# Last attention of a four-block network: ScalarE in place of GpSimd divides the probabilities of six of the 32 steps

## Chip, cores and metric

One core of one Trainium2 chip runs the whole program in one launch. The metric is the device time of that launch in microseconds (us), lower is better. The engines are TensorE (PE, with its weight loads as PEld), VectorE (DVE), ScalarE (ACT), GpSimd (POOL) and SyncE (SP), which issues DMAs. They run their own instruction lists and meet at semaphores.

## The reference, cut to what matters

Eight blocks follow each other on x of 4 x 256 rows by 256 columns; the change is in the seventh, the eighth comes behind it and its router is interleaved with the seventh.

```python
x = x + _L3_xattn_ref(_layernorm(x), ctx_2048, itok_BxS_0_1023, ...)   # 16 heads of 128
    scores = (q_nope . k_nope + q_rope . k_rope) * scale
    good = (k_ids <= qs) & (k_ids >= qs - LOOKBACK)                     # each query sees few keys
    attn = jax.nn.softmax(jnp.where(good, scores, NEG), axis=-1)        # exp, then divided by its sum
    out = einsum(attn, v); x += out @ W_o
x = x + _L3_ffn_ref(_layernorm(x), ...)      # 64 experts, each row goes to 8 of them:
    top_k of x @ gate_w, rows gathered by expert, silu(gate) * up, down, weighted sum
```

## The kernel before

The last attention (function `l3x`) makes 32 steps, each for two heads and 256 queries. It is a software pipeline over k = 0 to 73: every engine has a loop over k that says what it does at k, and all engines run through these loops side by side. In the text "step q" is an attention step (q = 0 to 31), and k is the position in the pipeline. A step is spread over some ten values of k:

- TensorE: the query of step q at k = 2q (18 matrix products, L349 to L351 reading `qch`), the scores at k = 2q + 3 (L2650), four transposes of the probabilities at k = 2q + 8 (`tensor_turn`, L2658), the product with the values at k = 2q + 9 (`tensor_out`, L2668), and the output projection at k = 2q + 11 (`tensor_y`, L349 to L351 reading `op6h`).
- VectorE: the rotary part of the query (L2750 to L2753), mask and row minimum of the scores (`vector_masked`, L2762), at k = 2q + 5 the reciprocals of the sums (`ri6n`, L2785), and the low part of the heads (L2776). For the last two steps (q = 30, 31; the constant OWN is 30) it also divides (L2789).
- ScalarE: copy of the query (L2710), exponentials in four pieces of 128 x 128, two at k = 2q + 3 and two at k = 2q + 4 (L2715), copy of the transposed probabilities from PSUM to SBUF (`pt6n`, L2728) at k = 2q + 8, and the high part of the heads (`op6h`, L2732) at k = 2q + 9.
- GpSimd: at k = 2q + 5 it waits for the reciprocals of step q and divides, that is, it multiplies four 128 x 128 pieces of `p6n` in place by `ri6n` (L2839), for q = 0 to 29. The probabilities lie in five buffers used in turn.

`tensor_turn(k)` waits for the division of its step; then `pt` is copied, and `tensor_out` waits for that copy. In the order of TensorE only the scores of a later step stand between the transposes and `tensor_out`.

Between these the router of the eighth block runs for each of four groups of 256 rows as the rows of x get done: groups 0 to 2 inside this stage. For group g it starts at k = 26 + 16g: normalization (VectorE, with `rs` of L396 on GpSimd), transposes (L3242), copy `hT` on ScalarE (L3249), router logits on TensorE (L3273), mask `mk` and slots on VectorE, counts on TensorE (L3298 to L3303), row weights on VectorE (L3394). GpSimd then scatters the rows of the group to the experts' slots in HBM, with 16 indirect DMAs per group (`gpsimd_scatters`, L3357, `slots_in`): the table of the loop puts one or two of them at each k from 38 for group 0 and from 54 for group 1, behind the division of that k. In order, five scatters fall on two steps of attention. The 32 scatters of groups 2 and 3 follow from k = 70 on and in the next stage (`head`), where TensorE runs dense experts; then the gathered experts start, once all 64 scatters have landed.

Of the kernel before, what the change touches and what calls it, by code (L numbers as in the profile page):

```python
# [14 lines left out]
ACT = mybir.ActivationFunctionType  # L15
# [19 lines left out]
OWN = 30  # L35
# [2545 lines left out]
def l3x(nc, io, m, sig):  # L2581

    T, V, A, G, B = nc.tensor, nc.vector, nc.scalar, nc.gpsimd, m.B
    prev_norm = m.norm
    x = m.x = sig("x", NT)
    done = m.xfinal = lambda t: x.at(t + 1)
    m.next_norm = Norm(nc, m, sig, rows=m.row7[:, :, 0:D])
    r, w7 = m.router, m.weights = Router(nc, io, m, sig), Weights(nc, io, m, sig)
    done = m.xfinal
# [4 lines left out]
    sc, mn, ri, tr, pt, pn = [sig(n, c) for n, c in (  # L2594
        ("scores", 32), ("masked", 64), ("recip", 32), ("probs_T", 32), ("probs_T_sbuf", 32), ("probs_p", OWN))]
    ex, pnv = sig("exps", 64), sig("places", 32 - OWN)
    pv, oh, ol, y = [sig(n, 32) for n in ("heads", "heads_hi", "heads_lo", "heads_out")]
    m.heads_read = ol.at(32)
    m.queries_done, m.y_done = qlat.at(32), y.at(32)
# [2 lines left out]
    def routing(k):  # L2602

        g = (k - 26) // 16
        return g, k - 25 - 16 * g
# [28 lines left out]
    def tensor_score(k):  # L2634
# [15 lines left out]
                    i = T.matmul(B[2 + s][:, c], m.Q6[k % 2][r, j, c], K[r, w], start=(j == 0), stop=(j == 1))  # L2650
        i.then_inc(sc.sem, 1)

    def tensor_turn(k):
        T.wait_ge(*(pn.at(k + 1) if k < OWN else pnv.at(k + 1 - OWN)))
        if k >= 1:
            T.wait_ge(*pt.at(k))
        for i in range(4):
            r = T.transpose(B[4][:, i * 128:i * 128 + 128], m.p6n[k % 5][:, i, :], m.ident[:])  # L2658
        r.then_inc(tr.sem, 1)
# [23 lines left out]
    def tensor():  # L2683
        for k in range(74):
            if 0 < k < 64 and k % 2 == 0:
                tensor_query(k // 2)
            if k in (69, 70, 71):
                beat(T, m, B[1][:, 256:384], 3)
            if 8 <= k < 72 and k % 2 == 0:
                tensor_turn(k // 2 - 4)  # L2690
            if 3 <= k < 67 and k % 2:
                tensor_score((k - 3) // 2)
            if 9 <= k < 73 and k % 2:
                tensor_out((k - 9) // 2)
            if k >= 11 and k % 2:
                tensor_y((k - 11) // 2)
            if k >= 26:
                g, ago = routing(k)
                if g == 0 and ago == 5:
                    T.wait_ge(*m.joined.at(4))  # L2700
                if ago == 5:
                    r.tensor_turn(g, bank)
                if ago == 7:
                    r.tensor_logits(g, bank)
                if ago == 9:
                    r.tensor_count(g, bank)

    def scalar_query(q):
        A.wait_ge(*qlat.at(q + 1))
        A.copy(m.Q6[q % 2][:, 1, :], B[1][:, 0:256]).then_inc(qlh.sem, 1)  # L2710

    def scalar_exp(q, s):
        A.wait_ge(*mn.at(2 * q + s + 1))
        for i in (2 * s, 2 * s + 1):
            a = A.activation(m.p6n[q % 5][:, i, :], m.sc6n[q % 3][:, i, :], ACT.Exp, bias=m.mn6n[q % 5][:, i:i + 1],  # L2715
                             scale=-1.0, accum_out=m.su6n[q % 5][:, i:i + 1])
        a.then_inc(ex.sem, 1)

    def scalar():
        for k in range(74):  # L2720
            if 64 <= k < 67:
                scalar_exp((k - 3) // 2, (k - 3) % 2)
            if 0 < k < 64 and k % 2 == 0:
                scalar_query(k // 2)
            if 8 <= k < 72 and k % 2 == 0:
                q = k // 2 - 4
                A.wait_ge(*tr.at(q + 1))
                A.copy(m.pt6n[q % 3][:].rearrange("p s n -> p (s n)"), B[4][:]).then_inc(pt.sem, 1)  # L2728
            if 9 <= k < 73 and k % 2:
                q = (k - 9) // 2  # L2730
                A.wait_ge(*pv.at(q + 1))
                A.copy(m.op6h[q % 2][:], B[6][:, 0:256]).then_inc(oh.sem, 1)  # L2732
            if 3 <= k < 64:
                scalar_exp((k - 3) // 2, (k - 3) % 2)
            if k >= 26:
                g, ago = routing(k)
                if ago == 6:
                    r.scalar_turned(g, bank)
                if ago == 9:
                    r.scalar_exps(g)  # L2740
                if ago == 11:
                    r.scalar_high(g)
            if k in (12, 16, 20, 24):
                w7.scalar_high(k // 4 - 3)
# [86 lines left out]
    def gpsimd():  # L2831
        r.gpsimd_small()
        for k in range(74):
            if 5 <= k < 5 + 2 * OWN and k % 2:
                q = (k - 5) // 2
                G.wait_ge(*ri.at(q + 1))
                for i in range(4):
                    p = m.p6n[q % 5][:, i, :]
                    a = G.tensor_scalar(p, p, m.ri6n[q % 5][:, i:i + 1], 1.0, ALU.mult, ALU.mult)  # L2839
                a.then_inc(pn.sem, 1)  # L2840
            if k in (13, 17, 21, 25):
                w7.gpsimd_low(k // 4 - 3)
            if k == 24:
                r.gpsimd_places()
            if k >= 26:
                g, ago = routing(k)
                if ago == 2:
                    r.norm.gpsimd_rstd(g)
                if ago >= 13:
                    r.gpsimd_scatters(g, ago - 13)  # L2850
                elif g:
                    r.gpsimd_scatters(g - 1, ago + 3)

    return {"tensor": tensor, "scalar": scalar, "vector": vector, "gpsimd": gpsimd, "sync": sync}


# [1152 lines left out]
def program(nc, io, ctx):  # L4009
    m, sig = Mem(), Signals(nc, ctx)  # L4010
    memory(nc, ctx, m)
    m.slots_used = True
    stages(nc, io, m, sig, l0x, keys, l3p, l3x)
    for engine in (nc.scalar, nc.gpsimd, nc.tensor, nc.sync, nc.vector):
        engine.wait_ge(*m.fit.at(1))
    fit = nc.values_load(m.fit7[0:1, 0:1], min_val=0, max_val=1)
    value = reached(dict(sig.value))
    with nc.If(fit == 1):
        for part in few(nc, io, m, sig).values():
            part()  # L4020
    sig.value = {name: value.get(name, 0) for name in sig.sems}
    with nc.Else():
        for part in again(nc, m, sig).values():
            part()
        m.slots_used = False
        stages(nc, io, m, sig, l0x_wide, keys_wide, l3p_wide, l3x_wide)
        for part in every(nc, io, m, sig).values():
            part()
# [131 lines left out]
```

## Time and profile before

| | us |
|---|---|
| median of 3 runs | 686.11 (685.12 to 688.25) |
| profiled execution | 685.7 |
| its span | 683.0 |
| TensorE busy | 609.0 (89%) |
| VectorE busy | 523.7 (77%) |
| ScalarE busy | 428.1 (63%) |
| GpSimd busy | 363.0 (53%) |

The profiled execution's time is 2.7 us above its span (what lies before the first and after the last instruction). Starts are counted from the start of the span. The attention stage runs from about 300 to 446 us. "Idle before" in a row is the time that the engine stood still ahead of that instruction, and the name behind the arrow is what ended it.

### The profile page before, as it was taken

What the parts mean: (1) busy time and instruction counts of PE and PEld (TensorE: products, weight loads), DVE (VectorE), ACT (ScalarE), POOL (GpSimd) and SP (SyncE); (2) the same over time, 40 slices, a digit from 0 to 9 for tenths busy, and PEclk for the clock granted to TensorE, in tenths of its full rate; (3) what the DMA queues carried; (4) which work ended last, traced back from release to release, by engine and by line L of the source; (5) the groups of instructions that cost most, each with busy time, mean ns of one, the idle gap of its engine ahead of it and who ended that gap; (6) DMA issues with size and microseconds to landing.
All of it is one profiled execution on the core that took longest, in us unless ns stands there. A gap on an engine that the chain in (4) does not pass through costs nothing.

```text
span 683.0 us, 14285 instructions
## 1 busy us (share of the span) xinstructions
PE 609.0 (89%) x4996; PEld 508.8 (74%) x5000; DVE 523.7 (77%) x1534; ACT 428.1 (63%) x1150; POOL 363.0 (53%) x524
## 2 busy tenths in 40 slices
PE   3998979898899879989999999897799989988877
PEld 3977867776589834668888878675599888888764
DVE  6494489989856788687778988778778878878466
ACT  3635578949745368767776666452358878868430
POOL 6615848964600225435543888677405665666620
PEclk9999999999999999999999999999799999999998
DMA  8999023200010050039300112534448878876384
GB/s 318 334 300 300 27 58 106 82 2 1 4 47 1 0 231 1 2 95 368 114 2 10 66 67 83 183 135 154 159 146 280 261 263 292 282 251 216 133 344 168
DMA packets 47701, 100.50 MB, mean 147 GB/s; under 512 B 7390, under 2 KB 27951, under 8 KB 46246
## 3 DMA queue, kind: packets, MB, share of 16 engines
q1 hardware_dynamic: 40374, 82.33, 36.0%
q0 software_dynamic: 7248, 17.18, 6.8%
q8 instruction: 42, 0.69, 0.4%
q14 instruction: 37, 0.30, 0.2%
HBM read 60.04 MB, written 43.12 MB: 151 GB/s over the span
## 4 chain that ended last, share of the span: by engine, by line
PE 59%; DVE 19%; POOL 8%; ACT 7%; issue 6%; another core or an unknown queue 0%; DMA 0%; DVEq 0%; ACTq 0%; POOLq 0%
PE bank L349 13%; PE bank L351 12%; PE bank L350 11%; PE bank L2650 4%; PE bank L3707 3%; PE bank L2668 3%; PE bank L2658 2%; POOL hl L1238 2%; DVE st L382 2%; DVE HN L402 2%; DVE pt L1451 1%; DVE nm L1459 1%; PE bank L3790 1%; PE bank L1574 1%; POOL raw L1329 1%
## 5 line engine op out<-in xcount | busy, mean ns | idle before, releaser
L3946 POOL DMA_INDIRECT rows_out<-ye,di x87 | 91.4, 1051 | 65.0 <-issue 19.3
L3357 POOL DMA_INDIRECT slots_in<-row,si x64 | 65.6, 1026 | 25.1 <-issue 17.2
L349 PE MATMUL bank<-x7h,w7h 128*96 128x192 f32 x232 | 63.0, 272 | 10.5 <-DVE h L3885 5.7
L2839 POOL TENSOR_SCALAR p6n<-p6n,ri6n 128x128 f32<-128x128 f32 x120 | 46.1, 401 | 46.2 <-DVE ri6n L2785 45.8
L349 PE MATMUL bank<-w7h,h7h 96*128 96x256 f32 x164 | 49.7, 303 | 14.8 <-DVE X L3496 9.4
L351 PE MATMUL bank<-x7h,w7l 128*96 128x192 f32 x232 | 59.1, 255 | 0.3 <-issue 0.2
L350 PE MATMUL bank<-x7l,w7h 128*96 128x192 f32 x232 | 59.0, 254 | 0.0
L2715 ACT ACTIVATE p6n<-sc6n,mn6n 128x128 f32<-128x128 f32 x128 | 50.4, 397 | 10.8 <-DVE mn6n L2762 10.4
L396 POOL TENSOR_TENSOR rs<-ve,neghalf 128x2 f32<-128x2 f32 x32 | 23.1, 721 | 59.4 <-DVE ve L390 59.1
L3180 DVE TENSOR_TENSOR w7l<-w7f,w7h 128x640 fp32r<-128x640 f32 x60 | 49.5, 826 | 4.2 <-issue 2.3
L349 PEld LDWEIGHTS bank<-x7h,w7h 128*96 128x96 f32 x232 | 38.0, 164 | 13.9 <-DVE w7l L3180 8.9
L350 PE MATMUL bank<-w7l,h7h 96*128 96x256 f32 x164 | 47.6, 290 | 0.8 <-issue 0.8
L3803 ACT CAST x7h<-bank 128x384 fp32r<-128x384 f32 x58 | 27.8, 482 | 32.5 <-PE bank L3707 28.7
L351 PE MATMUL bank<-w7h,h7l 96*128 96x256 f32 x164 | 47.7, 291 | 0.0
L3175 ACT CAST w7h<-w7f 128x640 fp32r<-128x640 f32 x64 | 47.2, 740 | 0.0
L349 PEld LDWEIGHTS bank<-w7h,h7h 96*128 96x128 f32 x164 | 32.3, 197 | 16.5 <-DVE X L3496 7.7
L3813 ACT ACTIVATE ye<-bank,wd 128x256 f32<-128x256 f32 x87 | 38.8, 485 | 8.9 <-PE bank L351 7.0
L3846 DVE TENSOR_TENSOR x7l<-bank,x7h 128x384 fp32r<-128x384 f32 x58 | 31.7, 548 | 16.1 <-ACT x7h L3803 14.0
L2762 DVE CUSTOM_DVE_ANT_0 sc6n<-bank,nm 128x128 f32<-128x128 f32 x128 | 29.4, 285 | 13.6 <-PE bank L2650 13.6
L351 PEld LDWEIGHTS bank<-x7h,w7l 128*96 128x96 f32 x232 | 38.0, 164 | 0.3 <-issue 0.3
L350 PEld LDWEIGHTS bank<-x7l,w7h 128*96 128x96 f32 x232 | 38.1, 164 | 0.0
L1441 ACT ACTIVATE p<-bank,nm 128x256 f32<-128x256 f32 x64 | 29.6, 483 | 9.4 <-DVE nm L1459 9.2
(483 smaller groups left out, 2247.0 us busy)
## 6 DMA issues: line engine op xcount, KB each, us to landing
w7f<-in_w SPq DMA_DIRECT2D x64, 320.0 KB
xe<-slots_in SPq DMA_DIRECT2D x29, 432.0 KB
slots_in<-zt SPq DMA_DIRECT2D x7, 1728.0 KB, 17.9
rows_out<-zt SPq DMA_DIRECT2D x8, 1024.0 KB, 11.1
rw<-rows_out SPq DMA_DIRECT2D x3, 2048.0 KB
w0raw<-in_w SPq DMA_DIRECT2D x3, 768.0 KB
wo<-in_w_o SPq DMA_DIRECT2D x1, 2048.0 KB
raw<-in_w SPq DMA_DIRECT2D x2, 704.0 KB
```

The costliest lines, as they stand in the source:

```text
L349: T.matmul(out, lh, rh, start=first, stop=False, **kw)
L350: T.matmul(out, lh, rl, start=False, stop=False, **kw)
L351: return T.matmul(out, ll, rh, start=False, stop=last, **kw)
L1441: a = A.activation(m.p2[n][:, mc, :], B[2 * (k % 2) + i % 2][:, mc * 256:mc * 256 + 256], ACT.Exp, bias=m.nm2[n][:, mc:mc + 1], accum_out= ...
L2715: a = A.activation(m.p6n[q % 5][:, i, :], m.sc6n[q % 3][:, i, :], ACT.Exp, bias=m.mn6n[q % 5][:, i:i + 1], scale=-1.0, accum_out=m.su6n[q ...
L2839: a = G.tensor_scalar(p, p, m.ri6n[q % 5][:, i:i + 1], 1.0, ALU.mult, ALU.mult)
L3175: A.copy(self.high(e)[:], self.whole(e)).then_inc(self.hi.sem, 1)
L3180: V.tensor_tensor(self.low(e)[:], self.whole(e), self.high(e)[:].bitcast(F32), ALU.subtract).then_inc(self.lo_v.sem, 1)
L3357: G.indirect_dma_start(out=m.buf_in, out_offset=bass.IndirectOffsetOnAxis(ap=m.si7[:, t, j:j + 1], axis=0), in_=m.row7[:, t, :], in_offset ...
L3813: A.activation(m.ye7[q % NY][:], out_bank(q), ACT.Copy, scale=m.wd7[:, 0, q:q + 1]).then_inc(ye.sem, 1)
L3846: V.tensor_tensor(m.x7l[j % 3][:, c, :], B[c][:, 0:2 * CAP], m.x7h[j % 3][:, c, :].bitcast(F32), ALU.subtract).then_inc(xl.sem, 1)
L3946: G.indirect_dma_start(out=m.buf_out, out_offset=bass.IndirectOffsetOnAxis(ap=m.di7[:, q:q + 1], axis=0), in_=m.ye7[q % NY][:], in_offset= ...
```

## The change

Six steps, q = 18, 20, 22, 24, 26 and 28, are divided by ScalarE, with four activations (Copy with a scale per row) at k = 2q + 6, right behind the exponentials of that k. GpSimd leaves out its division there. The transposes of a step wait for whichever engine divides it, by a semaphore of its own for ScalarE.

```diff
+    by_scalar = tuple(range(18, OWN, 2))
+    pna = sig("probs_scalar", len(by_scalar))
...
+    def normalized(k):
+        if k >= OWN:
+            return pnv.at(k + 1 - OWN)
+        done = sum(q <= k for q in by_scalar)
+        return pna.at(done) if k in by_scalar else pn.at(k + 1 - done)
+
     def tensor_turn(k):
-        T.wait_ge(*(pn.at(k + 1) if k < OWN else pnv.at(k + 1 - OWN)))
+        T.wait_ge(*normalized(k))
...
                 scalar_exp((k - 3) // 2, (k - 3) % 2)
+            if k % 2 == 0 and (k - 6) // 2 in by_scalar:
+                q = (k - 6) // 2
+                A.wait_ge(*ri.at(q + 1))
+                for i in range(4):
+                    a = A.activation(m.p6n[q % 5][:, i, :], m.p6n[q % 5][:, i, :], ACT.Copy,
+                                     scale=m.ri6n[q % 5][:, i:i + 1])
+                a.then_inc(pna.sem, 1)
...
-            if 5 <= k < 5 + 2 * OWN and k % 2:
+            if 5 <= k < 5 + 2 * OWN and k % 2 and (k - 5) // 2 not in by_scalar:
```

GpSimd's order from step 17 on (buffer `p6n2` is step 17, `p6n3` 18, `p6n4` 19, `p6n0` 20, `p6n1` 21, `p6n2` 22, `p6n3` 23; "DMA slots_in" are the scatters of group 0), before:

```order
L2839 TENSOR_SCALAR p6n2_299<-p6n2_299,ri6n2_314 128x128 x4
L3357 DMA slots_in<-row7_364,si7_381 13312x288 x2
L2839 TENSOR_SCALAR p6n3_300<-p6n3_300,ri6n3_315 128x128 x4
L3357 DMA slots_in<-row7_364,si7_381 13312x288 x3
L2839 TENSOR_SCALAR p6n4_301<-p6n4_301,ri6n4_316 128x128 x4
L396 TENSOR_TENSOR rs_59<-ve_58,neghalf_55 128x2
L3357 DMA slots_in<-row7_364,si7_381 13312x288 x2
L2839 TENSOR_SCALAR p6n0_297<-p6n0_297,ri6n0_312 128x128 x4
L3357 DMA slots_in<-row7_364,si7_381 13312x288 x3
L2839 TENSOR_SCALAR p6n1_298<-p6n1_298,ri6n1_313 128x128 x4
```

and now:

```order
L2854 TENSOR_SCALAR p6n2_299<-p6n2_299,ri6n2_314 128x128 x4
L3372 DMA slots_in<-row7_364,si7_381 13312x288 x5
L2854 TENSOR_SCALAR p6n4_301<-p6n4_301,ri6n4_316 128x128 x4
L396 TENSOR_TENSOR rs_59<-ve_58,neghalf_55 128x2
L3372 DMA slots_in<-row7_364,si7_381 13312x288 x5
L2854 TENSOR_SCALAR p6n1_298<-p6n1_298,ri6n1_313 128x128 x4
```

The scatters of two steps, which stood as two and three between divisions, now stand as five in a row; the same happens from step 21 to 23 and from 25 to 29.

ScalarE's order at k = 62 to 64, the last place of the change, before:

```order
L2728 COPY pt6n0_317<-bank4 128x512
L2715 ACTIVATE p6n4_301,su6n4_311<-sc6n2_296,mn6n4_306 128x128 x2
L2732 CAST op6h1_285<-bank6 128x256
L2715 ACTIVATE p6n0_297,su6n0_307<-sc6n0_294,mn6n0_302 128x128 x2
L3249 COPY hT32_363<-bank5 128x2x256
L2715 ACTIVATE p6n0_297,su6n0_307<-sc6n0_294,mn6n0_302 128x128 x2
```

and now:

```order
L2736 COPY pt6n0_317<-bank4 128x512
L2723 ACTIVATE p6n4_301,su6n4_311<-sc6n2_296,mn6n4_306 128x128 x2
L2747 ACTIVATE p6n3_300<-p6n3_300,ri6n3_315 128x128 x4
L2740 CAST op6h1_285<-bank6 128x256
L2723 ACTIVATE p6n0_297,su6n0_307<-sc6n0_294,mn6n0_302 128x128 x2
L3264 COPY hT32_363<-bank5 128x2x256
L2723 ACTIVATE p6n0_297,su6n0_307<-sc6n0_294,mn6n0_302 128x128 x2
```

The division of step 28 (L2747) stands ahead of the high part of the heads, two exponentials and the router's copy `hT`. At the other five places it stands likewise between the exponentials and `op6h`. The orders of TensorE, VectorE and SyncE are the same as before.

## Rows read from the trace of the kernel before

**Rows 1.** The page: engines' busy time, and the chain that ended last
```profile
PE 609.0 (89%) x4996; PEld 508.8 (74%) x5000; DVE 523.7 (77%) x1534; ACT 428.1 (63%) x1150; POOL 363.0 (53%) x524
...
PE 59%; DVE 19%; POOL 8%; ACT 7%; issue 6%; another core or an unknown queue 0%; DMA 0%; DVEq 0%; ACTq 0%; POOLq 0%
```
**Rows 2.** Three stretches: PE, PEld, DVE, ACT, POOL busy (instructions), TensorE clock, DMA
```profile
305.00:372.00 67.00, 67.00 (x648) 56.41 (x646) 51.57 (x248) 50.09 (x189) 32.44 (x78) 1.00 0.39 134
372.00:440.00 68.00, 63.37 (x582) 52.34 (x579) 58.04 (x269) 43.41 (x165) 55.35 (x87) 0.97 0.29 100
```
**Rows 3.** TensorE's waits, 375 to 445 us: total, times, longest
```profile
PE bank L2668 <- ACT pt6n L2728: 2.5, 4, 0.9
PE bank L3298 <- DVE mk L3288: 1.8, 1, 1.8
PE bank L3273 <- ACT hT L3249: 0.4, 1, 0.4
...
PEld bank L2658 <- POOL p6n L2839: 0.2, 1, 0.2
```
**Rows 4.** Chain of work, 396 to 407 us: start, length, what
```profile
398.73 1.09 PE bank L2650 x16
...
402.13 0.12 PE bank L350
402.25 1.61 PE bank L351
403.86 0.02 issue
403.89 0.37 ACT Q L2710
404.26 0.50 ACT pt6n L2728
404.75 0.04 issue
404.80 0.65 PE bank L2668 x4
```
**Rows 5.** GpSimd in order of time: start, length, instruction, [idle before]
```profile
378.54 1.42 POOL L2839 TENSOR_SCALAR p6n<-p6n,ri6n 128x128 f32<-128x128 f32 x4 [0.16 <-DVE ri6n L2785]
...
400.35 1.05 POOL L3357 DMA_INDIRECT slots_in<-row,si  x1 [0.17 <-issue]
...
402.97 0.96 POOL L3357 DMA_INDIRECT slots_in<-row,si  x1 [0.30 <-issue]
...
430.89 1.42 POOL L2839 TENSOR_SCALAR p6n<-p6n,ri6n 128x128 f32<-128x128 f32 x4
...
437.63 0.96 POOL L3357 DMA_INDIRECT slots_in<-row,si  x1 [0.30 <-issue]
441.73 0.96 POOL L3357 DMA_INDIRECT slots_in<-row,si  x1 [3.14 <-DVE row L3394]
```
**Rows 6.** ScalarE in order of time where step 28's division will stand
```profile
425.74 0.39 ACT L2715 ACTIVATE p6n<-sc6n,mn6n 128x128 f32<-128x128 f32 x1
426.03 0.19 ACT L2715 ACTIVATION_READ_ACCUMULATOR p6n<-sc6n,mn6n 128x1 f32 x1
426.98 0.37 ACT L2732 CAST op6h<-bank 128x256 fp32r<-128x256 f32 x1 [0.76 <-PE bank L2668]
...
428.03 0.57 ACT L3249 COPY hT<-bank 128x512 f32<-128x512 f32 x1
```
**Rows 7.** ScalarE: `op6h` behind steps 18, 20, 22, 24, 26, with its idle time
```profile
382.16 0.37 ACT L2732 CAST op6h<-bank 128x256 fp32r<-128x256 f32 x1 [1.14 <-PE bank L2668]
...
390.70 0.37 ACT L2732 CAST op6h<-bank 128x256 fp32r<-128x256 f32 x1 [0.76 <-PE bank L2668]
...
400.77 0.35 ACT L2732 CAST op6h<-bank 128x256 fp32r<-128x256 f32 x1
...
409.68 0.37 ACT L2732 CAST op6h<-bank 128x256 fp32r<-128x256 f32 x1 [0.40 <-PE bank L2668]
...
417.77 0.37 ACT L2732 CAST op6h<-bank 128x256 fp32r<-128x256 f32 x1 [0.32 <-PE bank L2668]
```
**Rows 8.** TensorE in order of time, steps 28 and 29
```profile
427.68 0.60 PE L2658 MATMUL bank<-ident,p6n 128*128 128x128 f32 x4
428.65 1.10 PE L3273 MATMUL bank<-rg,hT 128*128 128x64 f32 x8 [0.37 <-ACT hT L3249]
...
432.37 0.66 PE L2658 MATMUL bank<-ident,p6n 128*128 128x128 f32 x4
434.87 0.48 PE L3298 MATMUL bank<-base,ones 1*128 1x128 f32 x2 [1.84 <-DVE mk L3288]
```
**Rows 9.** Chain of work, 426 to 446 us
```profile
429.75 1.86 PE bank L2650 x16
...
438.06 1.68 PE bank L2658 x4
```
**Rows 10.** VectorE in the next stage, where scatters run without a break
```profile
488.09 0.88 DVE L3496 SCALAR_TENSOR_TENSOR X<-bank,wt,X 128x256 f32<-128x256 f32 x2 [2.43 <-PE bank L351]
```

## Prediction

> **What bounds the kernel now.** I read the page first [rows 1]: TensorE is busy for 609.0 of 683.0 us and makes 59% of the chain that ended last; ScalarE (63% busy, 7% of the chain) and GpSimd (53%, 8%) have room on the average. An average says little of one stage, so next come the stretches [rows 2]. From 305 to 372 us, attention without scatters, TensorE is busy for 67.00 of 67.00 us: nothing else matters there. From 372 to 440 us, where the scatters run and all six changed steps lie, it is busy for 63.37 of 68.00, so 4.6 us stand open. GpSimd is the busy one beside it: 55.35 of 68.00 us, against 32.44 of 67 before. ScalarE has 43.41 of 68.
>
> Then the waits of TensorE [rows 3], which say who owns those 4.6 us. The division on GpSimd is waited for once, by a weight load, for 0.2 us. The rest is 2.5 us in four waits of `tensor_out` for the copy `pt6n`, 1.8 us once for the router's mask `mk` on VectorE, 0.4 us once for the router's copy `hT` on ScalarE. So the work that the change takes off GpSimd is nearly never what TensorE waits for.
>
> What makes `pt6n` late is not ScalarE's own load either. The chain [rows 4] shows one of the four: matmuls follow each other at 0.12 us, but the last one of the query stands with 1.61 us, until 403.86; only then can ScalarE copy `Q` and `pt6n`, and TensorE goes on at 404.80. TensorE's own end signal came some 1.5 us late. There is nothing of this in the 67.00 full microseconds before the first scatter, and at 400.35 to 403.9 GpSimd is issuing scatters [rows 5]. The scores at 429.75 are drawn out likewise, 1.86 us in place of 1.09 [rows 4, 9], and the transposes at 438.06 with 1.68 us. I call these **late signals**. They come while GpSimd issues scatters; the rows do not say by which path.
>
> **The change part by part.**
>
> *GpSimd, removed:* six divisions of 1.42 us [rows 5], 8.5 us of its 55.35. TensorE waits for none of these six. Step 29's division, which stays, is the one behind the 0.2 us wait: it starts at 430.89 and its transposes follow at 432.37 [rows 5, 8]. Without step 28's division ahead it starts up to 2 us earlier. That buys nothing: TensorE's next work at 434.87 waits for `mk` for 1.84 us anyway [rows 8], so 0.2 us more of idle time go there. The scatters of group 1, which end at 438.6 now, end some 2 us earlier; group 2 starts at 441.73 and waits 3.14 us for the row weights of VectorE [rows 5]. Credit: 0.
>
> *ScalarE, added:* four activations of 128 x 128 per step. No row shows a Copy with a scale per row on this shape. The exponential on the same shape lasts 0.39 us, and its follower starts 0.29 us behind it [rows 6]. I take 0.30 us each, since they follow back to back, so 1.2 us per step; bounds are 0.26 (nothing but a shorter start) and 0.39 each (no overlap), 1.0 to 1.6 us per step. The page ScalarE: Activation LUTs of the Trainium skill (Rules for kernel authors) speaks against the change: it gives multiplications to VectorE and budgets about 0.3 us per activation and 0.83 ns per element. As an estimate from that page a step is 4 x 0.41 = 1.6 us, and the sum below would be +0.9 in place of +0.45. The row's 0.29 us from start to start decides for me.
>
> What hides the 1.2 us: the division stands between the exponentials and `op6h`, and there ScalarE stands idle for 1.14, 0.76, 0, 0.40 and 0.32 us at steps 18 to 26 [rows 7], and 0.76 us at step 28 [rows 6]. So `op6h` comes 0.1 to 1.2 us later. `op6h` itself has time (its reader, `tensor_out` of the next step, is over 3 us away); the tight one is the copy `pt6n` behind it, which has 1.09 us of scores to hide its 0.50 us [rows 4]. Ahead of it lies ScalarE's second idle place, the wait for the query (part of the 0.4 to 2 us that it waits each step for TensorE). At steps 18, 20, 24 and 26 the rest, 0.1, 0.45, 0.8 and 0.9 us, ends there or in the 0.5 us of cover. At step 22 the whole 1.2 us stays, but the query of 402.25 is late by 1.5 us just there, so it is hidden too. Credit: 0 for five steps.
>
> At **step 28** something else stands behind the division: `hT`. TensorE waits for that copy already (0.37 us, [rows 8]), because at k = 64 no query is left to compute. `hT` starts at 428.03 and would start 1.2 - 0.76 = 0.45 us later; logits, scores, mask, counts follow from it one after the other. This is **+0.45 us** on the path.
>
> *The new wait of the transposes:* step 28's division ends on ScalarE at 426.22 + 1.2 = 427.4 us (426.22 is the end of the accumulator read [rows 6]), the transposes start at 427.68 [rows 8]. It holds by 0.25 us; behind it in TensorE's list stand the logits, which wait for `hT` later than that. With 0.39 us per piece it ends at 427.8 and costs nothing more.
>
> *Late signals:* scatters that stood as two and three between divisions now stand as five. Now the five pairs of steps with two-and-three cost, by the four waits of 2.5 us less the last one of 0.46 us, plus 0.77 us of the scores, 2.8 us in all, so 0.56 us per five scatters. The one existing run of five (432.48 to 438.6) costs 0.46 us: the wait behind the transposes of 438.06. Moved to that price the five pairs give 5 x (0.46 - 0.56) = **-0.5 us**. The bounds are far apart: all 3.3 us gone, or much more (below). The page SBUF — State Buffer of the Trainium skill (Who interferes with whom) says that a DMA never contends with a compute engine and that TensorE and ScalarE wait for no one. By that rule the grouping of scatters is worth nothing and the sum is +0.45. The rows speak against it at least for signals, 1.61 us in place of 0.12.
>
> *Everything else* (experts behind 446 us, blocks before 300 us) is unchanged in order. **Sum:** +0.45 - 0.5 = -0.05, about 0. On the profiled execution's 685.7 us that is 685.65, and the median of the runs stands 0.4 above it, so I predict **686.0 us** for the median. A measurement of this kernel can tell about 0.5%, 3.4 us, from no change.
>
> **The rivals.**
>
> *A, slower: longer runs of scatters hold TensorE's signals longer.* For it: in the next stage, where scatters follow each other without a break, VectorE waits 2.43 us for a matmul [rows 10] whose neighbours take a quarter of a microsecond. Against it: run of five at 432 to 438 cost only 0.46 us, and the ten scatters from 441.73 on hold nothing that the waits show. Place: `pt6n` and the masks from 378 to 431 us. Price: a signal held for 2.4 us leaves 2.4 - 0.6 = 1.8 us of stall (0.9 of 1.5 us came through at 404.80), against 0.56 now, so +1.26 us per run, five runs: +6.3 + 0.45, **692.9 us**. It decides as slower from three runs of five on (+4.2). Chance 0.14.
>
> *B, faster: fewer turns between division and scatter, no late signals.* The 3.3 us of stall go and `hT` costs 0.45: **683.2 us**. The half microsecond that TensorE would keep by not falling in speed behind its wait at 434.87 could add to it. For it: late signals are denser from 378 to 431 us than from 441 to 457. Against it: scatters are the same in number. Chance 0.11.
>
> *C, ScalarE becomes the bound.* With 1.6 us per step and no lucky late query, steps 20, 22, 24 and 26 overrun the cover of `pt6n` by 0.1 to 0.4 us each, and step 28 costs 0.85: +2.0 - 0.5, **687.6 us**. For it: no idle time ahead of `op6h` at step 22. Against it: ScalarE is busy for 64% of the stretch [rows 2], with 7.2 us more 75%. Chance 0.09.
>
> **How the numbers follow.** The forecast has 0.66. Its own range is 684.2 to 687.8 (late signals coming and going by one or two). With the rivals the range is 682.9 to 689.2: A is in it as long as two runs or fewer show it, B and C wholly. Faster by over 0.5%: half of B (when more than the stalls goes) and 0.01 of the forecast, 0.07. Slower: A from three runs on, 0.07, and 0.02 of the others, 0.09. Within 0.5%: 0.84.
>
> **What the profile after would show.** Four ACT activations `p6n<-p6n,ri6n` per changed step at about 0.3 us from start to start; `hT` of group 2 starting 0.4 to 0.5 us later against the transposes of step 28, and TensorE's wait for it 0.8 us in place of 0.4; no wait for POOL `p6n`; GpSimd idle ahead of its divisions of steps 19 to 29; waits for `pt6n` of 1.5 to 3.5 us in total. Wrong would be: waits for `pt6n` over 6 us (A) or under 1 us (B), or `pt6n` late with the query's signal on time (C).

## The result, and the profile after

| | before | changed |
|---|---|---|
| median of the runs | 686.5 us (685.12 to 688.25, 4 runs) | 698.89 us (698.04 to 700.84, 4 runs) |
| profiled execution, its span | 685.7, 683.0 us | 698.53, 695.8 us |
| ratio | | 1.0178, 95% interval 1.0146 to 1.0210 |

The change makes the kernel 12.4 us slower. The forecast was 686.0 us, with a range to 689.2. I start with the page of the changed kernel, to be held against [rows 1]:

```profile
PE 613.6 (88%) x4996; PEld 511.3 (73%) x5000; DVE 524.1 (75%) x1534; ACT 432.9 (62%) x1174; POOL 353.9 (51%) x500
...
PE 49%; DVE 22%; ACT 10%; POOL 8%; issue 7%; another core or an unknown queue 3%; DMA 0%; DVEq 0%; ACTq 0%; POOLq 0%
```

GpSimd has lost 9 us of work and ScalarE gained 5. Neither is near its limit. What is new is in the chain: 3% of it, 21 us, stand as "another core or an unknown queue" on a kernel with one core. That is time behind a signal which came after the instruction that raised it had ended.

Next the stretches of the changed kernel, for [rows 2], with two more (columns as there):

```profile
305.00:372.00 67.00, 66.94 (x646) 56.16 (x644) 51.52 (x247) 50.20 (x191) 32.59 (x78) 1.00 0.39 134
372.00:440.00 68.00, 59.09 (x507) 48.82 (x507) 50.68 (x233) 42.88 (x167) 37.98 (x55) 0.92 0.20 71
376.00:456.00 80.00, 67.56 (x572) 55.69 (x569) 57.70 (x259) 47.39 (x181) 42.56 (x59) 0.91 0.24 85
385.00:388.00 3.00, 3.00 (x16) 2.83 (x14) 2.29 (x9) 1.93 (x8) 2.81 (x6) 0.50 0.00 0
```

The last two of them in the kernel before:

```profile
376.00:456.00 80.00, 75.19 (x642) 60.94 (x639) 65.62 (x289) 49.38 (x169) 63.48 (x92) 0.98 0.31 108
385.00:388.00 3.00, 2.54 (x20) 2.16 (x21) 2.97 (x16) 2.41 (x10) 2.50 (x4) 1.00 0.07 24
```

Up to 372 us nothing differs. From 376 to 456 us TensorE is busy for 7.6 us less, and its granted clock is 0.91 in place of 0.98; just behind its first long wait it is 0.50, which is the lower of its two levels, 1.2 GHz. To see where it adds up I use one landmark, the transposes of step 31, the last of the attention. They start at 442.46 us before, and in the changed kernel at:

```profile
455.10 0.60 PE L2666 MATMUL bank<-ident,p6n 128*128 128x128 f32 x4
```

That is 12.6 us later. From there to the end both traces take the same, 240.5 and 240.7 us. So the whole loss arises in the stretch that the change touches. Over the same work, from 376 us to this landmark, TensorE is idle for 4.8 us before and 12.4 now, and busy for 61.7 and 66.7. So 7.6 us of the loss is idle time, and the other 5.0 us is the same work at the lower clock.

TensorE's waits from 375 to 456 us in the changed kernel, for [rows 3]:

```profile
PE bank L2676 <- ACT pt6n L2736: 8.6, 5, 3.2
...
PE bank L3313 <- DVE mk L3303: 2.0, 1, 2.0
...
PE bank L3288 <- ACT hT L3264: 1.2, 2, 0.8
...
PE bank L2666 <- ACT p6n L2747: 0.3, 1, 0.3
```

`pt6n` was 2.5 us. Two of the five waits make most of it: 3.2 us behind the first row of five scatters and 3.1 us behind the fourth; behind the second it is 1.2, behind the third 0.2. The first is shown here, and it is the model of them. GpSimd in the changed kernel, with five scatters where two, a division and three had been:

```profile
375.78 1.05 POOL L3372 DMA_INDIRECT slots_in<-row,si  x1 [0.17 <-issue]
...
380.94 1.21 POOL L3372 DMA_INDIRECT slots_in<-row,si  x1 [0.30 <-issue]
384.66 1.41 POOL L2854 TENSOR_SCALAR p6n<-p6n,ri6n 128x128 f32<-128x128 f32 x4 [2.51 <-DVE ri6n L2800]
```

TensorE and ScalarE at the same time:

```profile
378.75 0.60 PE L2666 MATMUL bank<-ident,p6n 128*128 128x128 f32 x4
...
380.06 0.39 PE L2652 MATMUL bank<-KL,Q 64*128 64x128 f32 x4
383.62 0.65 PE L2676 MATMUL bank<-pt6n,KC 128*64 128x256 f32 x4 [3.18 <-ACT pt6n L2736]
```

```profile
381.54 0.37 ACT L2718 COPY Q<-bank 128x256 f32<-128x256 f32 x1 [2.98 <-remote]
382.99 0.58 ACT L2736 COPY pt6n<-bank 128x512 f32<-128x512 f32 x1 [1.07 <-remote]
...
384.25 1.27 ACT L2747 ACTIVATE p6n<-p6n,ri6n 128x128 f32<-128x128 f32 x4
385.42 0.35 ACT L2740 CAST op6h<-bank 128x256 fp32r<-128x256 f32 x1
```

The transposes end at 379.35; `pt6n`, which needs nothing but them and a free ScalarE, starts at 382.99, 0.8 us behind the last scatter's end (382.15). From 378.56 to 382.99 ScalarE does nothing but the copy of `Q`, and its four new activations come only later, so they can't be the reason. The signal of the transposes was held for 3.6 us. "Remote" is how the profile names such a wait.

### The profile page after: what moved, and what is told of

Its sections match the earlier page's. It is cut to its first block, busy times and chain, and to the rows that moved or that the text cites. A ratio compares the mean times of both kernels' runs of the same rounds, so it can differ in the third digit from the quotient of the medians.

```text
span 695.8 us, 14285 instructions
## 1 busy us (share of the span) xinstructions
PE 613.6 (88%) x4996; PEld 511.3 (73%) x5000; DVE 524.1 (75%) x1534; ACT 432.9 (62%) x1174; POOL 353.9 (51%) x500
## 4 chain that ended last, share of the span: by engine, by line
PE 49%; DVE 22%; ACT 10%; POOL 8%; issue 7%; another core or an unknown queue 3%; DMA 0%; DVEq 0%; ACTq 0%; POOLq 0%
PE bank L349 11%; PE bank L351 10%; PE bank L350 9%; PE bank L2652 3%; PE bank L3722 3%; PE bank L2676 2%; DVE st L382 2%; POOL hl L1238 2%; DVE HN L402 1%; ACT ye L3828 1%; DVE w7l L3195 1%; PE bank L2666 1%; DVE pt L1451 1%; ACT p6n L2723 1%
## 5 line engine op out<-in xcount | busy, mean ns | idle before, releaser
L3961 POOL DMA_INDIRECT rows_out<-ye,di x87 | 94.4, 1085 | 60.6 <-issue 17.9
L2854 POOL TENSOR_SCALAR p6n<-p6n,ri6n 128x128 f32<-128x128 f32 x96 | 34.7, 378 | 60.1 <-DVE ri6n L2800 60.1
```

Source lines behind the costliest of these rows:

```text
L3961: G.indirect_dma_start(out=m.buf_out, out_offset=bass.IndirectOffsetOnAxis(ap=m.di7[:, q:q + 1], axis=0), in_=m.ye7[q % NY][:], in_offset= ...
```

## The experiments

**Is it ScalarE's load, or the gap in GpSimd's?** Four kernels, beside which the kernel before took 686.64 us.

`e1_fill` is the change, with a dummy in place of each division that went:

```diff
+            if k % 2 and (k - 5) // 2 in by_scalar:
+                G.wait_ge(*ri.at(q + 1))
+                for i in range(4):
+                    a = G.tensor_scalar(m.spare[n % 2][:, i, :], m.ident[:], m.ri6n[q % 5][:, i:i + 1], ...)
```

> ScalarE divides the six steps as in the change, and GpSimd, where its divisions were, multiplies a constant tile into a spare buffer that nobody reads, with the same wait for the reciprocals and the same four 128 x 128 instructions. So ScalarE's load is that of the change and the scatters stand again as two and three. Theory A (runs of five scatters hold TensorE's signals): back to the kernel before, 685 to 688 us, waits for pt6n 1.5 to 4 us in place of 8.6. Rival (ScalarE's load, or its division coming too late, is what costs): it stays at 697 to 700 us.

Measured: 686.76 us (10 runs), ratio 0.9996 (0.9971 to 1.0021). The whole loss is gone, with ScalarE's divisions still in place.

`e3_act` is the reverse: the kernel before, with four idle Copy activations on ScalarE at the same six places (`A.activation(m.spare[0][:, i, :], m.ident[:], ACT.Copy, scale=...)`).

> The kernel before, with four activations (Copy with a scale per row, 128 x 128, from a constant tile into a spare buffer) on ScalarE at each of the six places of the change; GpSimd divides everything as before. Theory A: 686 to 688 us, the 1.2 us are hidden but for some 0.5 us at step 28. Rival (ScalarE's load): 697 to 700 us.

Measured: 688.35 us (10 runs), 1.0003 (0.9978 to 1.0028). ScalarE's new load costs nothing that these runs can show; the interval leaves room for 1.9 us. (The ratios come with the measurement and are not always the quotient of the two medians, which is 1.0025 here.)

`e2_vector` gives the six divisions to VectorE (`if q >= OWN or q in by_scalar:` in its own division of the last steps), so that ScalarE has none and GpSimd the same rows of five.

> VectorE divides the six steps (one 128 x 512 instruction of 0.69 us each, as it does for the last two steps), ScalarE divides nothing, GpSimd is as in the change. Theory A: runs of five scatters are still there, 695 us or more. Rival (ScalarE's load): 684 to 688 us, like before.

Measured: 693.31 us, 1.0102 (1.0066 to 1.0138). The loss needs no ScalarE. It is smaller than the change's. TensorE's wait for `pt6n` is 4.2 us in four here, none over 1.3, and its clock at 385 to 388 us stays at 1.00. Its longest wait is 2.5 us, for `hT`. How much of this loss is VectorE's, which has six divisions more, this run does not tell.

`e4_one` gives ScalarE a single step: `by_scalar = (18,)`, so one row of five.

> The change for one step alone, q = 18: one run of five scatters in place of a two and a three. Theory A with a cost per run: about a fifth of the 12.4 us, 688 to 690 us, with one wait for pt6n of about 2 to 3 us at 380 to 385 us. Rival (ScalarE's load summed over six steps): a sixth, also about 688 us, but then the wait stands behind ScalarE's division and not ahead of it. If only the last place (hT, step 28) or a loss behind the attention counted: 686 us.

Measured: 694.63 us, 1.0118 (1.0078 to 1.0159). One row of five costs 8 of the 12.4 us. The first line is TensorE's wait, the second its window behind it (TensorE alone: busy, clock, DMA share, GB/s):

```profile
PE bank L2676 <- ACT pt6n L2736: 3.9, 2, 3.2
```

```profile
385.00:388.00 3.00, 3.00 (x16) 0.50 0.00 0
```

It is the same 3.2 us and the same half clock. Of the 8 us, 5.7 are there at the transposes of step 31 (448.19 us in this trace, 442.46 before): 2.8 us are more idle time of TensorE (all its waits from 375 to 456 us, 7.5 in place of 4.7), and 3.0 us is the same work at the lower clock. Up to here: the cause is GpSimd's row of scatters, and the first place alone costs more than half of the whole.

**A place where nothing happens.** Four more kernels, meant as doses.

`e5_quarter`: as `e1_fill`, but the dummy is one piece of 128 x 128 in place of four.

> The change, with a break of one 128 by 128 multiplication (a quarter of the division's work, an estimate of 0.36 us) on GpSimd at the six places where a division was, behind the same wait for the sums' reciprocals. If only the length of an unbroken run of scatters counts, and any pause lets TensorE's held signals through, this reads like the kernel before, 685 to 688 us. If the queue of signals needs the time that it takes after the last scatter in the change's trace (about 0.8 us), the break lets part of them through, and the time lies between, 689 to 696 us. If the wait for the reciprocals itself, and not the work, was the break, it would read 686 too, and the idle time of GpSimd ahead of the dummy shows it.

`e6_signals`: the kernel before, where TensorE raises three more signals in each step:

```diff
+    extra = sig("extra", 96)
...
-        mm3(T, B[0][:, 0:256], ..., True, True)
+        mm3(T, B[0][:, 0:256], ..., True, True).then_inc(extra.sem, 1)
```

> The kernel before, with three more signals of TensorE in each of its steps (after the first query product, the first half of the scores and the first half of the values), for which nobody waits; the arithmetic and all waits stay. Theory of a queue, in which TensorE's signals are let through about one per scatter while GpSimd issues scatters: nine signals a step in place of six make the queue longer, the signals that are waited for arrive later, and the kernel is slower with no change on GpSimd, 692 to 705 us. Theory of a hold in time (each signal is late by what is left of the run, whatever stands before it): no change, 685 to 688 us. An increment may also cost TensorE itself something; then the steps ahead of the scatters (before 372 us) lengthen as well.

`e7_even`: the kernel before, with one scatter in each half step; `e8_even_after`: the change with the same:

```diff
-        for i in range(min(16, step * 5 // 4), min(16, (step + 1) * 5 // 4)):
-            self.gpsimd_scatter(g, i)
...
+        elif step < 16:
+            self.gpsimd_scatter(g, step)
```

(The branch of this attention is shown. One scatter of group 2 more is left to the head stage, whose loop is moved by one.)

> The kernel before, with one scatter in each half step in place of five in four half steps: between two divisions stand always two scatters, never three, and four of them lie further back, the last ones in the head stage. Theory of the run's length: the holds get shorter, the waits of TensorE in the later half of the attention (4.7 us from 375 to 456 us in the kernel before) shrink to 2 or 3 us, and the kernel takes 683 to 686 us, unless the later scatters put the load of the gathered rows off, which would give back up to 3 us. Rival: the run of three is short enough already, 686 to 689 us.

> The change, with one scatter in each half step: where a division is gone, four scatters stand in a row in place of five. A dose between the two kernels. If the queue grows with the run, this takes 689 to 696 us; if there is a length past which the stall sets in all at once, it reads like the one kernel or like the other (686 or 699 us).

Measured: 656.9, 656.96, 656.61 and 656.1 us. All are within 0.2% of the kernel before (ratios 0.9993, 0.9999, 0.9999 and 0.9989), and the kernel before itself took **657.09 us** here, in 31 runs (655.2 to 659.3). The same program took 682 to 687 us in every other batch, and the record gives the same chip number, 9, for this batch and for the first four kernels. TensorE's waits from 375 to 456 us in `e7_even`:

```profile
PE bank L3298 <- DVE mk L3288: 1.4, 1, 1.4
PE bank L349 <- DVE op6l L2776: 0.9, 1, 0.9
PE bank L2668 <- DVE op6l L2776: 0.5, 1, 0.5
```

No wait for `pt6n` is left. I compared the end of every instruction that raises a signal with the time at which the trace has the signal. In the profiled execution of the kernel before, 96 of TensorE's 661 signals are recorded more than 0.3 us late. None of them lies before 377 us, and GpSimd issues its first DMA of the whole program at 372.9. Of the other engines no signal is recorded late. But in that trace nearly 200 signals of VectorE, over 180 of ScalarE, 50 of TensorE and 27 of GpSimd have no record of their own before the engine's next one. In most of these cases an instruction that waits on that semaphore started in between, so these look like gaps in the record and not like late signals. In `e5_quarter` to `e8_even_after` no signal at all is late, and at most six in a trace have no record. Their scatters take as long as before (1.04 us in `e5_quarter`). So the holding of signals is a state, there in this batch or not for all runs alike, and not a property of the program. Two windows in the experts stage show that the two states differ beyond the attention too: TensorE alone, `e7_even` first, then the kernel before:

```profile
490.00:640.00 150.00, 147.04 (x1329) 0.98 0.81 281
```

```profile
500.00:650.00 150.00, 135.78 (x1237) 0.99 0.71 234
```

The step-31 landmark is at 437.57 in `e7_even`, 4.9 us ahead of 442.46; the other 24.5 us of the difference in span come behind it. That held signals make all of these 24.5 us is not shown. For the change this batch says something plain: with its six divisions on ScalarE and rows of four or of two and three scatters, nothing is lost or won. The change as it is did not run here, so that its own rows of five cost nothing in this state is likely, not shown.

**Again, where signals are held.** Beside the next two kernels the kernel before took 682.43 us.

`e9_again` is the changed kernel once more.

> The change as it is, once more, beside the kernel before on one chip. The last four kernels ran where the kernel before takes 657 us and where no signal of TensorE, VectorE or ScalarE comes later than 0.3 us in the attention; the change was measured where it takes 686 us and many come late. If the held signals are the whole cause of the 12 us, the change costs nothing wherever the kernel before takes about 657 us (ratio 0.997 to 1.004), and 1.014 to 1.021 wherever it takes about 686 us. If something else is at work, the ratio is the same in both.

Measured: 691.49 us, 1.0151 (1.0093 to 1.0209): the loss is back. Not every stall comes back in its size. Behind the first row of five TensorE waits 1.6 us in place of 3.2, and its clock stays at 1.00 there; behind the fourth it is 3.0. From the transposes of step 17 to those of step 31 this trace takes 72.2 us, the first one of the same program 76.4, and the kernel before 63.4. One wait of one trace is good to a factor of two.

`e10_signals` is `e6_signals` once more.

> The kernel before with three more signals of TensorE in each step, as in e6_signals. Where the kernel before takes about 657 us it shows nothing again. Where it takes about 686 us: by the theory of a queue that lets about one signal through per scatter it is slower, 692 to 705 us; by the theory of a hold in time it stays at 685 to 688 us.

Measured: 682.11 us (10 runs), 1.0013 (0.9979 to 1.0047). Three more signals in each step change nothing. The theory that the signals stand in a queue which lets one through per scatter falls; in this trace four of TensorE's signals arrive within 0.2 us of each other, 0.6 to 0.8 us behind the end of a row. These were held together and let go together. Not all are: in the first row of the changed kernel four late signals arrive at 378.57, 380.08, 381.52 and 382.96 us, one behind each scatter, 0.5 to 0.9 us behind its end. So a signal can come through in the middle of a row, or be held to its end.

**How long a row, how long a break.** Four kernels, beside which the kernel before took 685.56 us.

`e11_quarter` and `e12_even_after` are `e5_quarter` and `e8_even_after` once more.

> As e5_quarter: the change, with one multiplication of 128 by 128 (0.38 us in that trace) on GpSimd where a division was. Where signals are held (the kernel before at 680 to 690 us): if any break is enough, the ratio is 0.997 to 1.004; if the held signals need the time that they took after the last scatter of a row (about 0.8 us), part of the loss stays, 1.005 to 1.013; if the length of the break doesn't matter at all but its work does, as the change, 1.015 to 1.02. Where nothing is held (657 us), no difference.

> As e8_even_after: the change, with four scatters in a row in place of five. Where signals are held: 1.005 to 1.013 if the loss grows with the row's length, 1.0 or 1.018 if it has a threshold.

Measured: 692.56 us, 1.0100 (1.0060 to 1.0140), and 691.96 us, 1.0093 (1.0062 to 1.0124). Both keep about half of the loss. For `e11_quarter` this means that a break of 0.38 us between two and three scatters does only half of what one of 1.42 us does. For `e12_even_after` it does not mean that four in a row cost half of what five do, for it carries a second change, a longer row at the end of the attention. From the transposes of step 17 to those of step 29, where its rows of four lie, it takes 56.3 us, the kernel before 53.3 and the changed kernel 65.7 (64.7 in `e9_again`): the rows of four cost a quarter of what the rows of five do. Another 3.1 us go between steps 29 and 31, where seven scatters stand in a row and TensorE then waits for 3.05 us:

```profile
441.81 1.12 PE L2676 MATMUL bank<-pt6n,KC 128*64 128x256 f32 x4 [3.05 <-issue]
```

The first row of four, in GpSimd's order, and the wait of TensorE behind it:

```profile
376.03 1.06 POOL L3372 DMA_INDIRECT slots_in<-row,si  x1 [0.17 <-issue]
...
379.93 0.96 POOL L3372 DMA_INDIRECT slots_in<-row,si  x1 [0.31 <-issue]
```

```profile
382.71 0.65 PE L2676 MATMUL bank<-pt6n,KC 128*64 128x256 f32 x4 [2.03 <-ACT pt6n L2736]
```

`e13_woven` weaves the first scatter of a half step into the division (`if i == 1 and early: r.gpsimd_scatter(*early[0])` between its heads).

> The kernel before, with the first scatter of each half step that has a division put between the second and the third head of that division, so that rows of two and three scatters become rows of one and two. The division's end, for which TensorE waits, comes 1.3 us later. If the length of the row is what holds the signals, TensorE waits less, 0.988 to 0.998 of the kernel before where signals are held; where nothing is held only the later division is left, 1.000 to 1.006. If each scatter holds by itself, whatever stands around it, it is 1.000 to 1.006 in both.

Measured: 687.69 us (10 runs), 1.0029 (1.0009 to 1.0049). Shorter rows do what they should: six of TensorE's signals are late in the attention in place of 22, and its waits for `pt6n` fall to 0.4 us from 2.5. But from step 17 to step 29 the trace takes 56.4 us in place of 53.3, with waits for other things, the division (1.0 us) and the router's normalized rows (1.4 us) among them, and only from step 29 to 31 it is ahead (6.6 in place of 10.1). The later division takes back what the shorter rows give.

`e14_even` is `e7_even` once more.

> As e7_even: the kernel before, with rows of two scatters, never three. Where signals are held: 0.993 to 0.999 by the theory of the row's length; by its rival, that three in a row are short enough already, 0.999 to 1.004.

Measured: 690.50 us, 1.0077 (1.0053 to 1.0101), against my expectation. But look where. The landmark of step 31 stands at

```profile
438.27 0.60 PE L2658 MATMUL bank<-ident,p6n 128*128 128x128 f32 x4
...
446.31 1.12 PE L2668 MATMUL bank<-pt6n,KC 128*64 128x256 f32 x4 [6.77 <-ACT pt6n L2728]
```

4.2 us ahead of the kernel before. Of that, 1.5 us was there before the first scatter; from step 17 on it is 2.7 us ahead (60.7 us in place of 63.4, and 59.0 in `e7_even`, where no signal is held). So rows of two hold nothing that TensorE waits for. Right behind it comes a stall of 6.8 us. GpSimd's order shows its row:

```profile
427.84 1.42 POOL L2839 TENSOR_SCALAR p6n<-p6n,ri6n 128x128 f32<-128x128 f32 x4
429.43 1.56 POOL L3357 DMA_INDIRECT slots_in<-row,si  x1 [0.17 <-issue]
...
437.78 0.96 POOL L3357 DMA_INDIRECT slots_in<-row,si  x1 [0.30 <-DVE row L3397]
...
443.19 0.96 POOL L3357 DMA_INDIRECT slots_in<-row,si  x1 [0.30 <-issue]
452.46 0.72 POOL L396 TENSOR_TENSOR rs<-ve,neghalf 128x2 f32<-128x2 f32 x1 [8.30 <-DVE ve L390]
```

Behind the last division eleven scatters stand in a row (my expectations say twelve). In the kernel before, the first scatter of group 2 waits 3.14 us for its row weights [rows 5], and that wait is a pause. Here the weights are there in time, the pause is gone, and the row runs on. From step 31 to the end this trace takes 251.7 us in place of 240.5: the stall of 6.8 us and some 4 us more, whose place is open.

**A version that beats both?** Beside these three the kernel before took 683.60 us, beside the last 686.42.

`e15_even_fill` adds dummies to `e14_even` behind the last division, `e16_even_wait` only `G.wait_ge(*m.y_done)` ahead of the head stage's scatters.

> e14_even with its twelve scatters in a row at the end of the attention broken up: a dummy multiplication of four heads on GpSimd in each of the five half steps that have no division any more, each behind TensorE's step, and the head stage's scatters only after the last step. Theory of the row's length: the 4 us that e14_even was ahead at the attention's last step stay, 0.990 to 0.998 of the kernel before. Rival: the later scatters of the head stage end later and give it back, 0.998 to 1.005.

> e14_even with one wait alone: the head stage's first scatter waits for the attention's last product. Without the dummies the row is seven scatters in place of twelve. By the theory the stall of 6.8 us shrinks to 2 to 4 us: 0.997 to 1.005 of the kernel before.

Measured: 691.25 us, 1.0102 (1.0072 to 1.0131), and 687.69 us, 1.0059 (1.0036 to 1.0082). In `e15_even_fill` the long row is gone and TensorE's waits for `pt6n` with it, and from step 17 to 31 it takes 59.6 us, nearly the 59.0 of `e7_even`. But GpSimd's queue now holds the norm's `rs` behind the paced dummies, so that TensorE waits for something else:

```profile
PE bank L3255 <- DVE row L403: 7.1, 1, 7.1
```

In `e16_even_wait` the wait stands behind `rs` in GpSimd's order, which comes later than the product it waits for. The edit does nothing, and the run is in truth a second one of `e14_even`. It did not come out alike: group 2's weights are 0.73 us late in this trace, so the row is seven, a short pause and four, and the longest waits of TensorE behind it are 3.5 and 2.5 us, not 6.8.

`e18_even_pause` puts the pause where it was meant, `if k == 70: G.wait_ge(*y.at(30))`.

> e14_even with one wait: GpSimd's first scatter of the third group (four scatters before the end of the attention) waits for TensorE's output product of two steps before the last. The row behind the last division is then six scatters and a pause in place of twelve. If the row's length decides, the stall of 6.8 us falls to 0 to 3 us, TensorE's last step starts at 438 to 440 us, and the kernel takes 0.992 to 0.999 of the kernel before. Rival: the later scatters hold TensorE in the attention's last steps or end later in the head stage, 0.999 to 1.006.

Measured: 690.33 us, 1.0066 (1.0043 to 1.0090). The row behind the last division is now seven scatters, and TensorE's longest wait is

```profile
PE bank L2668 <- ACT pt6n L2728: 5.2, 2, 5.0
```

The signal that mattered was that of step 30's transposes, raised at 434.1 us in the middle of the row and followed at 439.14 by `pt6n`; the pause stands behind the row and does nothing for it. No version of mine beats the kernel before where signals are held, and none of the four did where they are not.

`e17_out_fill` asks about the experts stage: a dummy of two pieces on GpSimd behind each of the 87 scatters of the output.

> The kernel before, with a dummy multiplication of two pieces of 128 by 128 (0.7 us together) on GpSimd behind each of the 87 scatters of the experts' output. Where signals are held, the experts stage is some 21 us longer than where none is (185.1 us from the first transposed slots to the end, 164.1 in e7_even's trace). If rows of two or three scatters there hold signals and a break of 0.7 us lets them through, this is faster, 0.975 to 0.995; if GpSimd's added work delays the scatters instead, it is slower, 1.00 to 1.02.

Measured: 715.78 us, 1.0477 (1.0435 to 1.0518). GpSimd in its order of time:

```profile
565.58 1.05 POOL L3947 DMA_INDIRECT rows_out<-ye,di  x1 [0.17 <-issue]
566.67 0.56 POOL L3954 TENSOR_SCALAR zt<-ident 128x128 f32<-128x128 f32 x2
567.40 1.05 POOL L3947 DMA_INDIRECT rows_out<-ye,di  x1 [0.17 <-PE bank L351]
```

The 0.56 us dummy leaves 0.8 us from one scatter's end to the next one's start, and with it no signal of TensorE is recorded late in the experts stage, where 66 are in the kernel before. So the break does its work here too, and the 32 us are lost by something else. A scatter with its dummy takes 1.8 us of GpSimd in place of 1.3, and from 520 to 640 us GpSimd is busy for 108.2 of 120 us (76.4 before). ScalarE then waits for the scatters to read the eight buffers that it writes the experts' output to, a wait that the kernel before does not show:

```profile
ACT ye L3814 <- DMA rows_out<-ye,di: 54.0, 42, 7.2
```

Of the two answers that were expected, it is the second, at more than twice its price.

## Why the prediction was wrong

**The step that failed** is the term "Late signals": "Moved to that price the five pairs give 5 x (0.46 - 0.56) = -0.5 us." It took the price of a row of five from the one such row in the kernel before, 432.48 to 438.6, and that row is no sample. It stands where the queries and scores have ended, and the one signal that TensorE then waits on, that of the transposes of 437.86, was raised at 438.91, behind the last scatter (438.59). It could be held only for that scatter's 0.8 us. In the body of the attention the transposes end with two scatters or more still to come (379.35 of a row to 382.15), and a row of five costs TensorE up to 3.2 us of idle time at once. All five together: 7.6 us of idle time and 5.0 us of lower clock, against -0.5 forecast.

**The rival that came true** is A, with the mechanism as it was put, but the price short on both counts. Its +1.26 us for each row (1.8 - 0.56 is 1.24) measured 7.6 / 5 = 1.5 us idle on the average, from none to 3.2; the clock was not in it at all. I had the half clock in view, as a small gain of rival B, and did not ask what a longer stall would do. The chance of 0.14 was too low: I let one row of one kind weigh as evidence against a mechanism that the same rows showed.

Point by point:
- ScalarE's price: right. 1.27 us for the four activations, 1.2 forecast, and no cost that can be seen (`e3_act`, 1.0003). Rival C falls with it.
- `hT`: right. The wait for it at step 28 is 0.8 us in place of 0.4, as forecast.
- The transposes behind ScalarE's division: forecast to hold by 0.25 us, in fact a wait of 0.3 us once.
- GpSimd's credit of 0: right as to its work. But its division was not only work: it was the pause in which the held signals came through. "Credit 0" should have been a debit.
- The rule of the Trainium skill (SBUF — State Buffer, Who interferes with whom), that TensorE and ScalarE wait for no one, was weighed against 1.61 us in one row, and I sided with the row. The runs bear that out where signals are held: 3.2 us of wait while nothing but a signal was missing. The section speaks of the ports to SBUF, and no run here shows a conflict at a port; late signals are another matter, and taking the rule to cover them was my reading. Where none is held, in `e5_quarter` to `e8_even_after`, the regroupings that were tried are worth nothing, as the rule would have it.

**What the row length does**, from the longest wait of TensorE in `tensor_out` (which needs `pt6n`) behind a row, one trace each (all where signals are held):

| scatters in a row | 2 | 2 and 3 | 4 | 5 | 7 | 11 |
|---|---|---|---|---|---|---|
| kernel | e14, to 430 us | before | e12 | changed, e4, e9; e2 | e18; e16; e12, end | e14, end |
| longest wait, us | none | 0.9 | 2.0 | 3.2, 3.2, 3.0; 1.3 | 5.0; 3.5; 3.05 | 6.8 |

The worst that was seen grows with the row, by about 1 us for each scatter, which takes 1.3 us itself. The same length can also cost much less: the changed kernel's five rows cost 3.2, 1.2, 0.2, 3.1 us and nothing. A signal that falls early into a row can be held to its end, so the length sets how bad it may get; which signal falls there sets how bad it gets.

**Left open:** what in the chip holds the signals, and why it does so in most batches and not in one; whether it is GpSimd's issuing or the scatters' data on its way, since the packets of the changed kernel's first row move from 377 to 383.5 us, through the whole time in which signals are late; why signals of VectorE and ScalarE are missing from the record in the same state; and how much of the loss the clock is by itself, since no kernel was run with TensorE kept busy through the stall.

## What to carry to other kernels

Before work is taken off an engine that issues DMAs, ask what that work separates. If "unknown" or "remote" waits appear in the chain of a kernel on one core, and an engine's ends and its followers' starts don't meet, find which engine issues DMAs at that time, and take the price of longer rows of them from the place where most signals are waited for, plus the clock behind the stall. And time the kernel before beside each batch: here one and the same program took 657 us in one batch and 682 to 687 in the others, over twice the size of the effect under study.

## What the runs showed of the hardware

- While GpSimd issues indirect DMAs back to back (0.96 to 1.05 us each, 0.30 apart), signals of TensorE can be held until mostly 0.4 to 1.5 us behind one of them, often the last of the row. No signal of VectorE, ScalarE or GpSimd is recorded late. TensorE's stall was up to 5.0 us behind seven, 6.8 behind eleven. It is there or not there by batch, with the same program and the same chip number.
- Three more signals in each step make no difference (`e10_signals`, 1.0013). A pause of 1.42 us on GpSimd between two rows takes the loss away (`e1_fill`, 0.9996), one of 0.38 us half of it (`e11_quarter`, 1.0100). With a break of 0.8 us behind every scatter no signal is late in the experts stage (`e17_out_fill`), at a price of 32 us, as GpSimd's time for a scatter goes from 1.3 to 1.8 us.
- TensorE's granted clock was 0.50 from 385 to 388 us, behind a wait of 3.2 us, in both traces with that wait (the changed kernel and `e4_one`), and 1.00 there in `e2_vector`, `e9_again` and `e12_even_after`, behind waits of 1.3, 1.6 and 2.0 us. The length of the wait alone does not decide: in the kernel before it was 0.50 from 437 to 439 us, behind one of 1.84 us (434.87).
